# TensorE's order in an attention turn: score tile, half of the max units, second score tile, other half, values

## The reference, cut to what matters

```
q, k, v = split_heads(x @ wq), split_heads(x @ wk), split_heads(x @ wv)
scores  = where(causal, einsum('bhqd,bhkd->bhqk', q, k), -inf)
attn    = softmax(scores / sqrt(8), axis=-1)
ctx     = einsum('bhqk,bhkd->bhqd', attn, v)
```

## Time and profile before

| | |
|---|---|
| median of three runs | 1156.01 us (1155.78 to 1160.44) |
| profiled execution | 1162.2 us |
| its span, first to last instruction | 1160.4 us |
| first attention layer's turns | 185.7 to about 572.7 us of the span |
| second attention layer's turns | 751.3 to about 1134 us |
| TensorE, VectorE, ScalarE busy | 91%, 84%, 57% of the span |

### The profile page before, as it was taken

One profiled execution on the slowest core, in us unless ns is written; L12 is line 12 of the kernel. 1 busy time (PEld: TensorE's weight loads), 2 busy tenths in 40 slices (PEclk: granted clock), 3 DMA queues, 4 the chain that ended last, 5 costly groups with the idle time before them and its releaser, 6 DMA issues.

```text
span 1160.4 us, 34497 instructions
## 1 busy us (share of the span) xinstructions
PE 1054.0 (91%) x14718; PEld 483.9 (42%) x14718; DVE 972.7 (84%) x2307; ACT 661.3 (57%) x852; POOL 100.6 (9%) x124
## 2 busy tenths in 40 slices
PE   4989968999999999999998857799999999999998
PEld 2545543333333333334557826333333333333446
DVE  7787579999999999988544866899999999998854
ACT  3322214566787778777523222246667777777784
POOL 1431010000000000000042252000000000000000
PEclk9999999999999999999998979799999999999999
DMA  5061052000000000000001032220000000000001
GB/s 166 2 255 72 28 163 67 3 2 3 2 2 2 3 3 3 2 3 3 2 30 46 29 91 82 74 57 3 2 3 3 2 3 2 3 2 3 3 3 38
DMA packets 29493, 36.68 MB, mean 32 GB/s; under 512 B 3694, under 2 KB 26388, under 8 KB 29084
## 3 DMA queue, kind: packets, MB, share of 16 engines
q1 hardware_dynamic: 27228, 29.22, 7.6%
q0 software_dynamic: 2112, 5.25, 1.7%
HBM read 15.29 MB, written 18.87 MB: 29 GB/s over the span
## 4 chain that ended last, share of the span: by engine, by line
PE 51%; DVE 38%; issue 5%; ACT 4%; DMA 1%; another core or an unknown queue 1%; POOL 0%; SPq 0%; DVEq 0%; ACTq 0%; POOLq 0%
DVE part_max L2174 28%; PE psum L1999 12%; PE psum L2020 11%; PE psum L1970 6%; PE psum L520 5%; PE psum L1648 2%; PE psum L1985 2%; ACT hidden L2113 2%; PE psum L2053 1%; PE psum L2026 1%; DVE xn L204 1%; PE psum L299 1%; PE psum L544 1%; PE psum L1247 1%; PE psum L1259 1%
## 5 line engine op out<-in xcount | busy, mean ns | idle before, releaser
L2174 DVE TENSOR_REDUCE part_max<-psum 128x1 f32<-128x512 f32 (+3 forms) x1120 | 675.2, 667 | 38.2 <-PE psum L2026 22.1
L2113 ACT ACTIVATE hidden<-psum 128x1024 f32<-128x1024 f32 (+3 forms) x640 | 539.0, 895 | 216.7 <-PE psum L1970 215.8
L2020 PE MATMUL psum<-k_slots,q_slots 128*32 128x512 f16 (+3 forms) x5120 | 390.7, 355 | 26.1 <-DVE part_max L2174 14.9
L1999 PE MATMUL psum<-hidden,v_aug 128*9 128x512 f32 (+3 forms) x2560 | 289.3, 528 | 0.1
L2020 PEld LDWEIGHTS psum<-k_slots,q_slots 128*32 128x32 f16 x5120 | 123.3, 95 | 283.9 <-DVE part_max L2174 200.7
L1970 PE MATMUL psum<-q_slots,k_slots 32*128 32x512 f16 (+3 forms) x1472 | 140.6, 328 | 9.3 <-ACT hidden L2113 7.5
L520 PE MATMUL psum<-parts,w_parts 128*128 128x512 f16 x384 | 91.4, 390 | 3.8 <-DVE parts L945 3.8
L2026 PE MATMUL psum<-ident_bf,later_keys 128*32 128x128 bf16 (+2 forms) x1408 | 91.2, 250 | 0.0
L1970 PEld LDWEIGHTS psum<-q_slots,k_slots 32*128 32x128 f16 x1472 | 42.2, 91 | 98.7 <-ACT hidden L2113 47.4
L1985 PE MATMUL psum<-later_keys,ident_bf 128*32 128x128 bf16 x2048 | 74.6, 222 | 3.1 <-DVE v_aug L344 1.4
L1999 PEld LDWEIGHTS psum<-hidden,v_aug 128*9 128x9 f32 x2560 | 61.5, 90 | 34.5 <-ACT hidden L2113 1.5
(11 more groups left out here) (284 smaller groups left out, 840.6 us busy)
## 6 DMA issues: line engine op xcount, KB each, us to landing
expert_regions<-k_slots SPq DMA_DIRECT2D x2, 4096.0 KB, 17.8
q_slots<-q_rows SPq DMA_DIRECT2D x8, 512.0 KB, 3.7
k_slots<-k_rows POOLq DMA_DIRECT2D x28, 128.0 KB, 4.1
q_slots<-in_L_ffn_W_dram SPq DMA_DIRECT2D x2, 1024.0 KB, 6.6
q_rows<-parts SPq DMA_DIRECT2D x6, 256.0 KB, 2.6
k_rows<-parts SPq DMA_DIRECT2D x6, 256.0 KB, 2.7
q_slots<-expert_regions SPq DMA_DIRECT2D x20, 64.0 KB, 1.8
sorted_rows<-xn SPq DMA_DIRECT2D x5, 256.0 KB, 2.3
```

Of the source, the lines that this page charges most:

```text
L1999: last = pe.matmul(psum[VW * h:VW * h + DH + 1, O_BANK, off:CH], v_aug[:, j, G * g + h, :], probs[:, (2 * n + h // 2) % NP, h % 2, off:CH] ...
L2020: last = pe.matmul(psum[rows32(m), bank, a * w:(a + 1) * w], q_slots[:, g, qb * P + m * SLOT:qb * P + (m + 1) * SLOT], k_slots[:, G * g + ...
L2113: act.activation(probs[:, tile % NP, :, off:CH], psum[:, bank:bank + 2, off:CH], ACT.Exp, scale=scale).then_inc(exp_done, 1)
L2174: dve.tensor_reduce(part_max[:, step_no[s] % 2, h0:h0 + heads, i, kc], psum[:, bank, 0:heads * w].rearrange("p (a k) -> p a k", a=heads), ...
```

## The change

Before, a turn sends both score tiles one right behind the other, then half of the items, the values of the quad before, then the other half. After, the second score tile (with its mask on the diagonal) stands between the halves, and the values come last. Nothing else is changed; the instructions are the same.

```
                     if q:
                         score_tile(q, 0)
-                        score_tile(q, 1)
-                    if q in diagonal:
-                        mask_tile(q, 1)
                     for item in items[:half]:
                         if dense and item == final:
                             dense.mask_of(pe, 0)
                         ring_item(item)
+                    if q:
+                        score_tile(q, 1)
+                    if q in diagonal:
+                        mask_tile(q, 1)
+                    for item in items[half:]:
+                        ring_item(item)
                     if previous:
                         values(previous)
-                    for item in items[half:]:
-                        ring_item(item)
```

## The result

The changed kernel takes 1253.24 us (1252.41 to 1253.63), the kernel before 1155.96 us in the same comparison: a ratio of 1.0815 (95% interval 1.0789 to 1.0840). Slower was right; 1211 us was forecast, with a range up to 1238, so of the 97 us only 55 were foreseen.

What follows compares the result with a forecast made beforehand. VectorE was taken to bound A and B, TensorE to be nearly full in C and D. 1.6, 12.8, 8.4 and 4.6 make 27.4 us a layer, 55 for two: from 1156.0 to 1211 us, range 1184 to 1238.

Steps and rivals of the forecast that it cites:

- TensorE's prices: TensorE durations read from the trace: lone score tile to unit 0.32 us, change from full-height to score matmul 0.10.
- The turn of 2.59 us: A turn with four units after the change: 2.19 + 0.40 = 2.59 us on TensorE.
- C: Attention layer, 40 turns after the first 96, three max units each; TensorE nearly full; 8.4 us longer a layer.
- D: Attention layer, last 24 turns, two to no max units each; TensorE nearly full; 4.6 us longer a layer.
- no clock term enters: All stretches of the attention layer: granted clock 1.00 (the 2.4 GHz level), so nothing was added for the clock.
- A: Attention layer, first 32 turns, about five max units each; VectorE the bound; 1.6 us longer a layer (0 to 3.2).
- A almost as long as before: Sign expected in the profile after: stretch A hardly longer, 1.6 us a layer forecast.
- B: Attention layer, 64 turns after the first 32, four max units each; VectorE the bound; 12.8 us longer a layer.
- the ring of three is empty: Rival, slower by much more: VectorE starves in B too, 0.40 and 0.27 in full, 56 us a layer, 1268; chance 0.08.
- Tile 1's wait for ScalarE: Second score tile's wait for an exponential, seen in C: up to 0.48 us, claimed to go with the change.

Runs made afterwards that it cites:

- last experiment: The kernel before, with tile 1 one unit later in every second turn of two or three units off the diagonal: 1159.13 us, ratio 1.0005.

## Why the prediction was right in its sign and wrong in its size

- **TensorE's prices held.** Scores to unit 0.32, two units with the change to scores 0.54, the values with the change 0.96: each is in the timelines above. The turn of 2.59 us stands in two kernels in which the loop is open, and the 12 diagonal turns of C grew by 0.28 each where 0.27 was forecast.
- **C and D came out in part by luck.** They grew by 17.5 and 12.1 us in the two layers, where 16.8 and 9.2 were forecast, but not term by term. The 17 three-unit turns of C without a transposition went from 2.14 to 2.43 us on the mean, 4.9 us where about 0.08 each was forecast: the 2.27 taken for them before was the mean of one pair of turns, and not all come out at the forecast 2.35 (the first turn below takes 2.37, the second 2.55). With only three units in a turn, no unit laps another of the same turn, but C's five turns with four units grew by 2.4 us. Against that, the forecast gave 0.50 to each of C's turns with a transposition, since TensorE "waits for no exponential" there; the three with "out" did wait, 0.53 each (last experiment), lost that wait, and fell from 3.48 to 3.12. And 4.0 of D's 12.1 us are the clock's (last section), of which the sum says that no clock term enters.

```profile
515.81 0.39 PE L1970 MATMUL psum<-q_slots,k_slots 32*128 32x512 f16 x2
...
518.18 0.39 PE L1970 MATMUL psum<-q_slots,k_slots 32*128 32x512 f16 x2
...
520.73 0.39 PE L1970 MATMUL psum<-q_slots,k_slots 32*128 32x512 f16 x2
```

- **The step that failed** is the one on A: a unit is written when its bank is read, "so VectorE then has at most three banks of 0.598 ahead of it, 1.79. So 0 to 0.2 us idle; I take 0.1". The stretch without a unit was right (1.50, and 0.45 until VectorE begins). Two things were wrong. A bank is not handed back at VectorE's rate of 0.598, but at the end of its read, 0.69 after it began, and 0.06 more pass until TensorE starts. And the wait was treated as one idle piece a turn instead of as a loop: because the late unit itself heads the next stretch without a unit, nothing catches up. A five-unit turn lost 3.36 - 2.99 = 0.37, not 0.1. The 16 turns of A off the diagonal grew by 5.7 us, where 1.6 was forecast, and its 16 diagonal turns, to which I gave nothing, by 4.4. The sign that I named for it, "A almost as long as before", came out false.
- **B: the same step left out.** "2.59 against 2.39, 0.20 each" compares the two engines' throughput and asks nothing about the ring. The loop gives 2.70: the 35 four-unit turns without a transposition grew by 0.31 each on the mean, from 2.32 to 2.63. All 44 turns off the diagonal grew by 15.5 us instead of 8.8, and the 20 diagonal ones by 5.9, 0.29 each for 0.2 forecast. A and B were forecast at 28.8 us for the two layers and took 63.0: that is 34 of the miss of 42 us. C and D have 3.6. The rest comes from the 6.2 us by which the profiled execution of before lay above its median, which the forecast took off, while the one of after (1252.9) lies at its median; nearly 2 us outside the turns go the other way.
- **The rival nearest to what the runs show** was "the ring of three is empty", 1268 us, at a chance of 0.08. Its price was wrong (the 0.40 and 0.27 in full: with VectorE out of the way the order costs 81 us, not 112), and the argument against it, that there are waits to absorb it, failed: A and B lost 63 us. It deserved a working of its own.
- **Tile 1's wait for ScalarE went**, as said: the row of 7.5 us in 19 waits has no successor after. In the turns of the earlier trace rows it was worth hardly more than the price of sparing it (2.58 us became 2.54 in the last experiment); in the second turns of the steps, where the forecast saw no wait, it was worth more.
- **What the forecast didn't have** is in D, besides the clock: with the pair apart, transpositions ("out", L2053) stand ahead of tile 1 and come too early for ScalarE's copy. All four kernels with every pair apart have 4.8 us of this wait in 5 places; all others 0.8 in one. The wait of the changed kernel on TensorE and ScalarE:

```profile
614.23 1.09 PE L2053 MATMUL psum<-ident,xn_t 128*128 128x128 f32 x4 [1.10 <-ACT xn_t L2122]
```

```profile
613.50 0.58 ACT L2122 COPY xn_t<-psum 128x512 f32<-128x512 f32 x1
```

## What to carry to other kernels

Where a producer laps a ring of few banks, a turn costs at least the longest stretch without a ring item plus one full round trip of a bank (start to read, the whole read, hand-back): add it up for every order and compare it with the throughput of both engines, and take the largest of the three. The length of a single instruction belongs in that sum, not the distance between successive ones. Spread the ring's items so that no more of them than banks stand between two long stretches without one: one unit moved behind the values was worth 32 us here with the tiles apart (4 of them the clock's), and 55 with the tiles together. What is moved has to be such a unit: where it was a transposition, the loop's loss stayed.

## What the runs showed of the hardware

- Successive maxima of 512 columns come 0.598 us apart, but one of them lasts 0.69, and its bank is written only after its end (0.06 later). That the bank is kept to the end is the kernel's semaphore. The Trainium skill, "PSUM — Partial Sum Buffer", section "PSUM bank collisions raise a hardware error", says that TensorE writing a bank while VectorE reads the same quadrant of it raises an error and is not stalled. No run here shows that.
- The granted clock fell in D of both layers. Windows of the changed kernel (us, busy PE, PEld, DVE, ACT, POOL, clock, DMA), two in the first layer and one in the second:

```profile
612.00:614.20 2.20, 1.13 (x30) 0.57 (x31) 1.93 (x11) 1.68 (x4) 0.00 (x0) 0.89 0.00 0
614.20:620.70 6.50, 6.47 (x76) 2.68 (x80) 3.38 (x20) 2.77 (x5) 0.00 (x0) 0.51 0.01 3
...
1211.50:1215.00 3.50, 3.50 (x37) 1.43 (x33) 0.94 (x2) 1.41 (x2) 0.00 (x0) 0.58 0.02 5
```

In the first layer, after the wait of 1.10 us at L2053, in a stretch in which TensorE was busy for 1.13 of 2.20 us, it ran for 6.5 us at about half of the full clock, the 1.2 GHz level; in the second layer the same happened for about 3 us after a wait of 0.92 us at L2053. The turn with the wait and the next one take together 7.16 us in the first layer and 6.81 in the second; in the kernel with tiles apart and one unit behind the values they take 4.67 and 5.29, so that the clock cost 2.5 and 1.5 us. But that kernel has the same wait of 1.10 us after the same stretch, and its clock stayed at 1.00:

```profile
599.55:601.75 2.20, 1.14 (x30) 0.57 (x30) 1.93 (x11) 1.68 (x4) 0.00 (x0) 1.00 0.00 0
601.75:608.25 6.50, 5.38 (x92) 2.37 (x92) 3.54 (x21) 3.85 (x7) 0.00 (x0) 1.00 0.01 3
```

So the wait alone does not bring the clock down; what does is not shown.
